# Cross attention's keys: twelve head pairs by seven half products, alternating with four value units

## The chip, the core and the metric

One core of a Trainium2 chip runs the whole program. Times are device microseconds (us). Before the change three runs gave 1630.26, 1631.77 and 1633.85 us, median 1631.77. The engines are PE (TensorE, the matmuls), ACT (ScalarE), DVE (VectorE), POOL (GpSimd) and SP, whose queue issues every DMA.

## The reference, cut to what matters

The program is two layers (cross attention, gated feed forward, grouped attention, a LoRA layer). Only the start changes: the keys, values and queries of the first cross attention, for 8 x 128 = 1024 tokens, 32 heads of 128 and a model width of 512.

```python
x = _rmsnorm(hidden_states, ln_weight)          # hidden_states = _layernorm(x)
h_q = (x @ w_q.T).reshape(b, lq, H, DH)         # H = 32, DH = 128
h_k = (key_value_states @ w_k.T).reshape(b, lk, H, DH)
h_v = (key_value_states @ w_v.T).reshape(b, lk, H, DH)
score = jnp.einsum('bqhd,bkhd->bhqk', h_q, h_k) + position_bias[None]
...
x = x + _L0_xattn_ref(_layernorm(x, axis=-1), ctx_4096, ...)
```

## The kernel before, in words

**Three matmuls for one.** Every float32 product is made of three passes in a rounded format (`product`, L55 to L57): an operand is a pair, `hi` (rounded, a copy on ACT) and `lo` (what is left, a subtraction on DVE or POOL), and the passes are lo x hi, hi x lo, hi x hi. Weights arrive by DMA in `rawA`, `rawB`, `rawV`, `rawO` (128 x 1024 float32 each); ACT writes `wt*_hi`, then POOL `wt*_lo`, and only then does PE use them. There is one buffer for each of the four kinds, so the next split waits until PE has used the last.

**The context stage.** The transposed context is the pair `c_cT`. Eight rounds (`context_round`, written out for 0 and 1, a hardware loop for 2 to 6, the last in pieces) make keys and values of four heads each. A round before has eight key units, four from `wtA` (one head pair) and four from `wtB` (the next), then eight value units (one for each batch, four heads wide, from `wtV` and `wtO`). Every unit is 4 x 3 = 12 matmuls of 512 columns into one PSUM bank. ACT copies key units to `c_k_kept` (`keep_keys`, L837), DVE value units to `c_v_kept` (`keep_value`, L1046), and SP stores both to memory for the later stage. All four banks of the units are shared by keys and values.

**The input.** In round 0 DVE takes the statistics of `resid` (L1026), centres (L1035), ACT scales (L853), PE transposes one batch behind each value unit (`turn_x`, L636), ACT and DVE make `xT_hi` and `xT_lo`. POOL makes the factors: `scale_of` for that scaling, and `twice_of` (five small operations, L1233 to L1241) for `add_hidden` on ACT (L863), which turns `resid` into twice the normalised input, at the end of round 1.

**Seven half products.** The queries of a head pair are made by Strassen's scheme already (`first_five`, `sixth`, `seventh`): the pair's weights and the tokens are halved both ways, four combinations of the weights are made by POOL (`combine`), four of the input once (`Twist`, `x_twist`), and seven half products of 6 matmuls each, some added in the bank, replace four units of 12. ACT copies one quarter twice, DVE forms the sums (`query_sum`, L1116).

**What sets the order.** Every engine has its own list of instructions, written out by hand in the functions `sync`, `tensor`, `scalar`, `vector` and `gpsimd`, and runs it strictly in that order; semaphores hold one engine back for another. So an instruction that waits holds everything behind it on its engine.

Of the kernel before, what the change touches and what calls it, by code (L numbers as in the profile page):

```python
# [19 lines left out]
ALU = mybir.AluOpType  # L20
# [46 lines left out]
class Core:  # L67
# [29 lines left out]
    def place_context(self):  # L97

        self.cT = self.pair(self.ctx, "cT", [P, DC, TOK])
# [156 lines left out]
class Twist:  # L256
# [3 lines left out]
    def __init__(self, core, ctx, tag, nth):  # L260
        self.core, self.nth = core, nth
# [16 lines left out]
    def difference(self, dve, n, of, less, step):  # L278
        dve.wait_ge(self.core.twist_steps, 8 * self.nth + step)
        dve.tensor_tensor(self.plain[n - 1][:, :, :], self.plain[of - 1][:, :, :], self.plain[less - 1][:, :, :],  # L280
                          ALU.subtract).then_inc(self.core.twist_steps, 1)

    def high(self, act, n, step):
        act.wait_ge(self.core.twist_steps, 8 * self.nth + step)
        self.core.nc.scalar.copy(self.parts[n - 1][0][:, :, :], self.plain[n - 1][:, :, :]).then_inc(self.core.twist_hi, 1)
# [19 lines left out]
def cross_attention_phase(core, io, kept, norm_row, after):  # L305
# [9 lines left out]
    with ExitStack() as ctx:  # L315
# [3 lines left out]
        twist = Twist(core, ctx, "x", 0)  # L319
# [27 lines left out]
        ctx_raw = [v_kept[:, h, :, :].rearrange("p b f -> p (b f)") for h in range(4)]  # L347
        ln_w = core.row
# [54 lines left out]
        K_UNITS, V_UNITS = 8 * QUADS, 8 * QUADS  # L403
        CTX_A, CTX_B, CTX_V = QUADS + 1, QUADS, QUADS
# [11 lines left out]
        def x_bank(b):  # L416
            return banks[:, 4 + b % 4, :].rearrange("p (c t) -> p c t", c=DC)
# [7 lines left out]
        def context_rounds(engine, body):  # L425
            body(0)
            body(1)
            with engine.Fori(2, QUADS - 1) as i:
                body(i)

# [7 lines left out]
        def sync(sp):  # L438
# [16 lines left out]
            def store_keys(i, which):  # L455
                sp.wait_ge(qk_copied, 8 * i + 4 * which + 4)
# [9 lines left out]
            def context_round(i):  # L466
                key_weights("A", 2 * i + 2, i + 2)
                key_weights("B", 2 * i + 3, i + 1)
                value_weights(i + 1, i + 1)
                if isinstance(i, int) and i == 0:  # L470
                    small()
                store_keys(i, 0)
                store_keys(i, 1)
                store_values(i, 0)
                store_values(i, 1)

            def small():
                sp.wait_ge(ctx_hi, 2 * DC)
                sp.wait_ge(ctx_lo, 2 * DC)
                for n in range(2):  # L480
                    sp.dma_start(kept["ctx"][n], f32(cT[n][:, :, :]).rearrange("p c t -> p (c t)")).then_inc(ctx_stored, DMA)
                sp.wait_ge(centred_ready, B)
# [81 lines left out]
        def tensor(pe):  # L564
# [4 lines left out]
            def key_unit(kind, i, u):  # L569
                h, half = u % 4 // 2, u % 2  # L570
                if u >= 4:
                    pe.wait_ge(qk_copied, 8 * i + u - 3)
                elif not isinstance(i, int) or i:
                    pe.wait_ge(vo_added, 8 * i + u - 3)
# [21 lines left out]
            def keys(kind, i, which):  # L596
                weights_ready(kind, i + 2 if kind == "A" else i + 1)
                for u in range(4 * which, 4 * which + 4):
                    key_unit(kind, i, u)
# [8 lines left out]
            def value_unit(i, b):  # L608
                if b >= 4:
# [2284 lines left out]
```

## Time and profile before

| what | value |
|---|---|
| median of three runs | 1631.77 us |
| the profiled execution, its own time | 1630.46 us |
| its span | 1628.7 us |
| granted TensorE clock | 1.0 over the whole span |
| busy share of the span: PE, DVE, ACT, POOL | 99%, 58%, 46%, 50% |
| context stage (rounds 0 to 7) on PE | from 6 us to about 348 us |

The profile comes from one execution, whose own time is the number to add to and take from. A busy share near one says that PE has nearly no gap left, so there time can only come from fewer or shorter matmuls, or from one of its few gaps; on the other engines an idle stretch costs nothing unless PE waits for them. Matmuls overlap, so the mean duration of one (about 390 ns) is longer than the distance between two starts, which is what a matmul costs.

### The profile page before, as it was taken

What the parts mean: (1) busy time and instruction counts of PE and PEld (TensorE: products, weight loads), DVE (VectorE), ACT (ScalarE), POOL (GpSimd) and SP (SyncE); (2) the same over time, 40 slices, a digit from 0 to 9 for tenths busy, and PEclk for the clock granted to TensorE, in tenths of its full rate; (3) what the DMA queues carried; (4) which work ended last, traced back from release to release, by engine and by line L of the source; (5) the groups of instructions that cost most, each with busy time, mean ns of one, the idle gap of its engine ahead of it and who ended that gap; (6) DMA issues with size and microseconds to landing.
All of it is one profiled execution on the core that took longest, in us unless ns stands there. A gap on an engine that the chain in (4) does not pass through costs nothing.

```text
span 1628.7 us, 24911 instructions
## 1 busy us (share of the span) xinstructions
PE 1613.7 (99%) x8584; PEld 1377.3 (85%) x8584; DVE 936.5 (58%) x1460; ACT 748.0 (46%) x1930; POOL 814.8 (50%) x628
## 2 busy tenths in 40 slices
PE   9999999999999999999989999999999999999999
PEld 7888888888888888888878887888898898889887
DVE  4621111126567666666669666776657656665675
ACT  5331111115455454554553333656546545554653
POOL 5222212237656566476459775554535535453445
PEclk9999999999999999999999999999999999999999
DMA  8544433323333233332332111110111111010011
GB/s 318 192 151 155 155 129 147 125 89 115 103 107 122 93 118 119 107 120 99 113 130 59 51 48 56 59 33 27 46 33 40 46 39 33 27 36 26 24 53 52
DMA packets 52108, 146.40 MB, mean 90 GB/s; under 512 B 7265, under 2 KB 12001, under 8 KB 51521
## 3 DMA queue, kind: packets, MB, share of 16 engines
q1 hardware_dynamic: 52032, 145.41, 25.8%
q8 instruction: 46, 0.75, 0.2%
q14 instruction: 30, 0.24, 0.0%
HBM read 107.64 MB, written 37.75 MB: 89 GB/s over the span
## 4 chain that ended last, share of the span: by engine, by line
PE 93%; DVE 3%; POOL 1%; DMA 1%; ACT 1%; issue 1%; SPq 0%; DVEq 0%; POOLq 0%; ACTq 0%
PE banks L55 26%; PE banks L57 26%; PE banks L56 26%; PE banks L2053 3%; PE banks L689 3%; PE banks L709 3%; PE banks L698 2%; PE banks L2060 2%; DMA resid<-in_x 1%; PE banks L223 0%; DVE stats L1026 0%; DVE resid L1703 0%; POOL rstd L195 0%; DVE stats L182 0%; PE banks L636 0%
## 5 line engine op out<-in xcount | busy, mean ns | idle before, releaser
L1046 DVE COPY c_v_kept<-banks 128x512 f32<-128x512 f32 x64 | 44.3, 692 | 252.6 <-PE banks L57 252.6
L2517 POOL TENSOR_TENSOR g_swapped<-g_swapped,rawB 128x512 f32<-128x512 f32 x80 | 103.2, 1293 | 171.1 <-ACT g_swapped L2199 171.1
L1297 POOL TENSOR_TENSOR x_probs<-x_probs,x_inv 128x512 f32<-128x512 f32 x64 | 66.7, 1042 | 170.8 <-DVE x_inv L1102 168.0
L903 ACT ACTIVATE x_probs<-x_probs,x_top 128x128 f32<-128x128 f32 x256 | 99.5, 390 | 92.2 <-DVE x_top L1093 92.2
L2347 DVE TENSOR_TENSOR g_turned_by<-banks,rawB 128x512 f32<-128x512 f32 x80 | 55.2, 690 | 87.6 <-ACT g_swapped L2199 87.6
L2511 POOL TENSOR_TENSOR g_probs<-g_probs,g_inv 128x512 f32<-128x512 f32 x64 | 67.7, 1081 | 74.6 <-DVE g_inv L2338 74.4
L55 PE MATMUL banks<-wtV_hi,g_att_lo 128*128 128x512 f32 x256 | 104.3, 407 | 0.0
L55 PE MATMUL banks<-xT_hi,wtO_lo 128*128 128x512 f32 x256 | 102.9, 402 | 0.0
L2198 ACT COPY g_swapped<-banks 64x512 f32<-64x512 f32 x80 | 46.7, 584 | 121.5 <-PE banks L57 114.9
L56 PE MATMUL banks<-wtV_lo,g_att_hi 128*128 128x512 f32 x256 | 100.3, 392 | 0.0
L57 PE MATMUL banks<-xT_hi,wtO_hi 128*128 128x512 f32 x256 | 100.2, 391 | 0.0
L56 PE MATMUL banks<-xT_lo,wtO_hi 128*128 128x512 f32 x256 | 99.9, 390 | 0.0
L57 PE MATMUL banks<-wtV_hi,g_att_hi 128*128 128x512 f32 x256 | 99.8, 390 | 0.0
L55 PE MATMUL banks<-wtO_hi,x_att_lo 128*128 128x512 f32 x240 | 96.2, 401 | 0.0
L1112 DVE TENSOR_TENSOR resid<-banks,resid 128x512 f32<-128x512 f32 x128 | 85.3, 685 | 17.6 <-PE banks L57 17.5
L57 PE MATMUL banks<-wtO_hi,x_att_hi 128*128 128x512 f32 x240 | 93.8, 391 | 0.0
L56 PE MATMUL banks<-wtO_lo,x_att_hi 128*128 128x512 f32 x240 | 93.4, 389 | 0.0
L1116 DVE TENSOR_TENSOR x_q<-banks,x_q 128x512 f32<-128x512 f32 x80 | 55.1, 688 | 59.7 <-PE banks L57 59.2
L2189 ACT ACTIVATE g_probs<-g_probs 128x128 f32<-128x128 f32 x256 | 75.7, 298 | 26.2 <-DVE g_probs L2333 26.2
L2333 DVE SCALAR_TENSOR_TENSOR g_probs<-g_probs,g_cap,rawB 128x512 f32<-128x512 f32 x64 | 77.5, 1213 | 17.6 <-ACT g_probs L2183 17.5
L1212 POOL TENSOR_TENSOR wtA_lo<-rawA,wtA_hi 128x1024 fp32r<-128x1024 f32 (+1 forms) x25 | 57.8, 2310 | 55.5 <-ACT wtA_hi L821 36.7
L2369 DVE TENSOR_TENSOR resid<-banks,resid 128x512 f32<-128x512 f32 x120 | 80.8, 674 | 6.1 <-PE banks L57 5.7
(334 smaller groups left out, 5037.4 us busy)
## 6 DMA issues: line engine op xcount, KB each, us to landing
kept_k<-c_k_kept SPq DMA_DIRECT2D x16, 1024.0 KB, 4.0
x_k<-kept_k SPq DMA_DIRECT2D x32, 512.0 KB, 4.1
kept_v<-c_v_kept SPq DMA_DIRECT2D x14, 1024.0 KB, 5.0
x_v<-kept_v SPq DMA_DIRECT2D x28, 512.0 KB, 4.0
rawA<-in_x_wQ SPq DMA_DIRECT2D x16, 512.0 KB, 4.6
rawO<-in_x_wO SPq DMA_DIRECT2D x16, 512.0 KB, 3.5
rawO<-in_g_wQ SPq DMA_DIRECT2D x16, 512.0 KB, 3.5
rawV<-in_g_wO SPq DMA_DIRECT2D x16, 512.0 KB, 3.4
```

What stands on the lines that cost most here:

```text
L55: pe.matmul(out, w[1], x[0], start=start, stop=False, skip_group_check=adds)
L56: pe.matmul(out, w[0], x[1], start=False, stop=False, skip_group_check=adds)
L57: return pe.matmul(out, w[0], x[0], start=False, stop=stop, skip_group_check=adds)
L903: e = nc.scalar.activation(probs[:, b, :], probs[:, b, :], ACT.Exp, bias=top[:, b:b + 1], accum_out=total[:, b:b + 1])
L1112: dve.tensor_tensor(resid[:, b, :], banks[:, out_bank(g, b), :], resid[:, b, :], ALU.add)\
L1212: return pool.tensor_tensor(wt[into][1][:, cut], raw[kind][:, cut], f32(wt[into][0][:, cut]), ALU.subtract)
L1297: pool.tensor_tensor(probs[:, part, :], probs[:, part, :], rows, ALU.mult).then_inc(probs_ready, 1)
L2189: e = nc.scalar.activation(probs[:, t, :], probs[:, t, :], ACT.Exp, accum_out=total[:, t:t + 1])
L2333: dve.scalar_tensor_tensor(part, part, cap[:, 0:1], wide(mask), ALU.mult, ALU.add)\
L2369: dve.tensor_tensor(resid[:, b, :], banks[:, out_bank(r, u, b), :], resid[:, b, :], ALU.add).then_inc(proj_free, 1)
L2511: pool.tensor_tensor(probs[:, quarter(j), :], probs[:, quarter(j), :], rows, ALU.mult)\
L2517: pool.tensor_tensor(part, part, sin[:, :].unsqueeze(1).to_broadcast([P, HB, P]), ALU.mult)\
```

## The change

**Keys.** The first two head pairs (round 0) and the last two (round 7) are made as before. For the twelve pairs between, the keys are made by seven half products from `wtA` and `wtB` together, with `c_twist`, four combinations of the context that DVE makes in round 0 (`key_differences`) in the memory where `x_twist` lies later. A round from 1 to 6 is now, twice over: seven half products of one pair with one value unit between the fifth and the sixth, then three value units. ACT makes two copies for a pair, DVE five sums (`key_sums`) where ACT made four copies. POOL makes the weight combinations (`combine`) once for each pair, and the weights of a pair are split after the sixth and seventh product of the pair before. The combinations of the input for the queries move from round 1 to the end of round 6 and the time of the last keys.

**Input.** Statistics and centring move behind the first value units on DVE, the scaling behind the eight key copies on ACT; four of the eight transposes stay in round 0 (behind values 4 to 7), four move into round 1. They use banks 6 and 7 where they used 4 to 7; the values of round 1 use banks 4 and 5, those of later rounds 4 to 7. `twice_of` and the mask's conversion (`mask_of`) move on POOL from the end of round 0 to the end of round 1.

**An address.** `cT`, the context as grouped attention reads it again, gets a gap in front, as `c_cT` has one: it starts on a line of 128 bytes now, and 96 bytes into one before.

```diff
     def place_context(self):
 
+        self.line_up(self.ctx, "cT_line")
         self.cT = self.pair(self.ctx, "cT", [P, DC, TOK])
...
+        SEVENS = PAIRS - 4
+        K_UNITS, V_UNITS = 8 + 7 * SEVENS + 8, 8 * QUADS
...
         def x_bank(b):
-            return banks[:, 4 + b % 4, :].rearrange("p (c t) -> p c t", c=DC)
+            return banks[:, 6 + b % 2, :].rearrange("p (c t) -> p c t", c=DC)
+
+        def key_step(i, which):
+            return 2 * i - 2 + which
...
# sync
             def context_round(i):
-                key_weights("A", 2 * i + 2, i + 2)
-                key_weights("B", 2 * i + 3, i + 1)
...
+                key_weights("A", 2 * i + 1, key_step(i, 1) + 2)
                 value_weights(i + 1, i + 1)
...
                 store_keys(i, 0)
+                key_weights("A", 2 * i + 2, key_step(i, 1) + 3)
+                store_values(i, 0)
...
                 store_keys(i, 1)
-                store_values(i, 0)
                 store_values(i, 1)
...
# tensor
+            def seven_keys(i, which):
+                n = key_step(i, which)
+                weights_ready("A", 2 + n + 1)
+                pe.wait_ge(qk_copied, 8 + 2 * n)
+                if isinstance(i, int) and i == 1 and which == 0:
+                    pe.wait_ge(vo_added, 8)
+                    key_twist.ready(pe, 4)
                 else:
-                    pe.wait_ge(qk_copied, 8 * i + 5 + b)
-                value_product(b, b % 4)
+                    pe.wait_ge(q_sums, 5 * n)
+                part(X, a11, c11)
+                part(Y, s2, ct2)
+                part(Z, s1, ct1)
+                pe.wait_ge(qk_copied, 8 + 2 * n + 1)
+                part(X, a12, c21, True)
+                pe.wait_ge(q_sums, 5 * n + 1)
+                part(Y, s3, ct3, True)
+                if which == 0:
+                    weights_ready("V", i + 1)
+                    weights_ready("O", i + 1)
+                value_unit(i, 4 * which)
+                if isinstance(i, int) and i == 1 and which == 0:
+                    turn_x(4)
+                pe.wait_ge(q_sums, 5 * n + 2)
+                part(Y, a22, ct4, True)
+                pe.wait_ge(q_sums, 5 * n + 3)
+                part(Z, s4, c22, True)
...
+                for which in range(2):
+                    seven_keys(i, which)
+                    for b in range(4 * which + 1, 4 * which + 4):
+                        value_unit(i, b)
+                        if isinstance(i, int) and i == 1 and which == 0:
+                            turn_x(b + 4)
...
# scalar
+            def seven_weights(n, loads, a_used, b_used):
+                act.wait_ge(raw_in["A"], DMA * loads)
+                act.wait_ge(w_steps, 4 * n + 2)
+                act.wait_ge(qk_made, a_used)
+                nc.scalar.copy(wt["A"][0][:, :], raw["A"][:, :])
+                act.wait_ge(w_steps, 4 * n + 4)
+                act.wait_ge(qk_made, b_used)
+                nc.scalar.copy(wt["B"][0][:, 0:6 * P], raw["B"][:, 0:6 * P]).then_inc(w_hi["A"], 1)
+
+            def key_weights(n):
+                seven_weights(n, n + 2, products_before(n - 1) + 6, products_before(n))
...
+                value_weights(i)
...
+                key_copy(i, 0)
...
+                key_quarter(i, 0)
...
+                key_weights(key_step(i, 0) + 1)
...
+                key_copy(i, 1)
+                key_quarter(i, 1)
...
+                    key_weights(key_step(i, 1) + 1)
                 if second:
-                    twist.high(act, 2, 6)
-                    twist.high(act, 4, 8)
                     for b in range(B):
                         add_hidden(b)
-                value_weights(i + 1)
...
# gpsimd
             def context_round(i):
...
+                value_weights(i)
+                for which in range(2):
+                    n = key_step(i, which) + 1
...
+                        combine(n, n + 2, ("A", n + 2))
+                        seven_low(n + 3)
+                if isinstance(i, int) and i == 1:
                     twice_of()
-                    pool.wait_ge(mask_in, DMA)
-                    pool.wait_ge(qk_made, 4)
-                    pool.tensor_scalar(mask, mask8, MASKED, -MASKED, ALU.mult, ALU.add).then_inc(mask_ready, 1)
-                value_weights(i + 1)
+                    mask_of()
```

How the lists move at three places, before first and the changed one second. A name ahead of `<-` is written, those behind it are read; in brackets stand the semaphores that it waits for.

**ACT in round 0**, from the last weights of the start to the first transposed input: `c_k_kept` are the key copies, `s_centred` the input.

```order
L821 CAST wtO_hi<-rawO 128x1024 [waits x_raw_inO]
L837 COPY c_k_kept<-banks 128x512 [waits x_qk_made] x4
L821 CAST wtA_hi<-rawA 128x1024 [waits x_raw_inA,x_qk_made]
L853 ACTIVATE s_centred<-s_centred,s_scale 128x512 [waits s_centred_ready,s_scale_ready] x4
L837 COPY c_k_kept<-banks 128x512 [waits x_qk_made] x4
L821 CAST wtB_hi<-rawB 128x1024 [waits x_raw_inB,x_qk_made]
L858 CAST xT_hi<-banks 128x4x128 [waits s_x_turned]
```

```order
L915 CAST wtO_hi<-rawO 128x1024 [waits x_raw_inO]
L928 COPY c_k_kept<-banks 128x512 [waits x_qk_made] x4
L292 CAST c_twist_hi<-c_plain 128x1024 [waits twist_steps] x2
L928 COPY c_k_kept<-banks 128x512 [waits x_qk_made]
L292 CAST c_twist_hi<-c_plain 128x1024 [waits twist_steps] x2
L928 COPY c_k_kept<-banks 128x512 [waits x_qk_made] x3
L961 CAST wtA_hi<-rawA 128x1024 [waits x_qk_made,x_w_steps,x_raw_inA]
L964 CAST wtB_hi<-rawB 128x768 [waits x_qk_made,x_w_steps]
L983 ACTIVATE s_centred<-s_centred,s_scale 128x512 [waits s_centred_ready,s_scale_ready] x4
L988 CAST xT_hi<-banks 128x4x128 [waits s_x_turned] x3
```

The scaling of the input stood between the first four key copies and the last four; now it stands behind all eight, and behind the first split for the seven products.

**ACT from the end of round 1 into round 2** (the branch and the ISA row are the loop's start): `resid` is `add_hidden`, `wtV_hi` and `wtO_hi` the value weights of round 2.

```order
L821 CAST wtB_hi<-rawB 128x1024 [waits x_raw_inB,x_qk_made]
L285 CAST x_twist_hi<-x_plain 128x1024 [waits twist_steps] x2
L863 ACTIVATE resid<-resid,s_mean_scaled,s_twice 128x512 [waits s_twice_ready] x8
L821 CAST wtV_hi<-rawV 128x1024 [waits x_raw_inV,x_vo_made]
L821 CAST wtO_hi<-rawO 128x1024 [waits x_raw_inO]
L428 UNCONDITIONAL_BRANCH
L428 ISA
L836 ISA [waits c_k_stored0]
L837 COPY c_k_kept<-banks 128x512 [waits x_qk_made]
```

```order
L955 COPY c_k_kept<-banks 128x512 [waits x_qk_made]
L961 CAST wtA_hi<-rawA 128x1024 [waits x_qk_made,x_w_steps,x_raw_inA]
L964 CAST wtB_hi<-rawB 128x768 [waits x_qk_made,x_w_steps]
L993 ACTIVATE resid<-resid,s_mean_scaled,s_twice 128x512 [waits s_twice_ready] x8
L451 UNCONDITIONAL_BRANCH
L451 ISA
L914 ISA [waits x_vo_made]
L915 CAST wtV_hi<-rawV 128x1024 [waits x_raw_inV]
L915 CAST wtO_hi<-rawO 128x1024 [waits x_raw_inO]
L949 REGISTER_ALU
L950 ISA [waits c_k_stored0]
L951 COPY c_k_kept<-banks 128x512 [waits x_qk_made]
```

The value weights of round 2 stand behind `add_hidden` in both; the key weights that `add_hidden` stands behind are other ones, and the first key copy of round 2 follows the value weights as before.

**POOL around `twice_of`** (`rstd`, `s_mean_scaled`, `s_twice`): in round 0 before, at the end of round 1 now.

```order
L1212 TENSOR_TENSOR wtA_lo<-rawA,wtA_hi 128x1024 [waits x_w_hiA]
L1212 TENSOR_TENSOR wtB_lo<-rawB,wtB_hi 128x1024 [waits x_w_hiB]
L1233 TENSOR_SCALAR var_eps<-moments 128x8 [waits s_scale_ready]
L1235 TENSOR_TENSOR rstd<-var_eps,power 128x8 [waits s_scale_steps]
L1237 TENSOR_TENSOR var_eps<-moments,rstd 128x8 [waits s_scale_steps]
L1239 TENSOR_SCALAR s_mean_scaled<-var_eps 128x8 [waits s_scale_steps]
L1241 TENSOR_SCALAR s_twice<-rstd 128x8 [waits s_scale_steps]
L1259 TENSOR_SCALAR normed<-row 128x1024 [waits x_qk_made,x_mask_in]
```

```order
L1428 TENSOR_TENSOR wtA_lo<-rawA,wtA_hi 128x1024 [waits x_w_hiA]
L1509 TENSOR_TENSOR wtB_lo<-rawB,wtB_hi 128x768
L1445 TENSOR_SCALAR var_eps<-moments 128x8 [waits s_scale_ready]
L1447 TENSOR_TENSOR rstd<-var_eps,power 128x8 [waits s_scale_steps]
L1449 TENSOR_TENSOR var_eps<-moments,rstd 128x8 [waits s_scale_steps]
L1451 TENSOR_SCALAR s_mean_scaled<-var_eps 128x8 [waits s_scale_steps]
L1453 TENSOR_SCALAR s_twice<-rstd 128x8 [waits s_scale_steps]
L1458 TENSOR_SCALAR normed<-row 128x1024 [waits x_qk_made,x_mask_in]
L451 UNCONDITIONAL_BRANCH
L451 ISA
L1428 TENSOR_TENSOR wtV_lo<-rawV,wtV_hi 128x1024 [waits x_w_hiV]
L1428 TENSOR_TENSOR wtO_lo<-rawO,wtO_hi 128x1024 [waits x_w_hiO]
```

The five small operations stood behind splits of round 0; now they are the last but one thing of round 1, behind the low parts of the weights of its last pair (`wtA_lo`, `wtB_lo`).

## Rows read from the trace of the kernel before

**Rows 1.** The page, part 1: busy us of each engine, share of the span, instructions.

```profile
PE 1613.7 (99%) x8584; PEld 1377.3 (85%) x8584; DVE 936.5 (58%) x1460; ACT 748.0 (46%) x1930; POOL 814.8 (50%) x628
```

**Rows 2.** The waits of PE, whole span: us in total, times, longest.

```profile
PE banks L55 <- ACT c_k_kept L837: 2.4, 1, 2.4
```

**Rows 3.** Timeline of PE, end of round 0's keys: start us, us, engine, line, operation.

```profile
29.08 0.39 PE L57 MATMUL banks<-c_cT_hi,wtB_hi 128*128 128x512 f32 x1
...
31.89 0.47 PE L55 MATMUL banks<-wtV_hi,c_cT_lo 128*128 128x512 f32 x1 [2.42 <-ACT c_k_kept L837]
...
34.70 0.60 PE L636 MATMUL banks<-ident,s_centred 128*128 128x128 f32 x4
```

**Rows 4.** Timeline of ACT, rounds 0 and 1: scaling the input, adding the hidden.

```profile
28.56 2.71 ACT L853 ACTIVATE s_centred<-s_centred,s_scale 128x512 f32<-128x512 f32 x4 [3.50 <-DVE s_centred L1035]
...
82.89 5.75 ACT L863 ACTIVATE resid<-resid,s_mean_scaled,s_twice 128x512 f32<-128x512 f32 x8
```

**Rows 5.** Timeline of DVE, rounds 0 and 1.

```profile
22.44 2.48 DVE L1026 BATCH_NORM_STATS2 stats<-resid 128x6 f32<-128x512 f32 x4 [9.01 <-DMA resid<-in_x]
...
27.74 2.71 DVE L1035 SCALAR_TENSOR_TENSOR s_centred<-resid,moments,row 128x512 f32<-128x512 f32 x4
...
57.33 0.69 DVE L1046 COPY c_v_kept<-banks 128x512 f32<-128x512 f32 x1 [1.46 <-PE banks L57]
...
60.12 7.22 DVE L275 TENSOR_TENSOR x_plain<-xT_hi,xT_lo 128x1024 f32<-128x1024 f32 x3
67.26 3.48 DVE L280 TENSOR_TENSOR x_plain<-x_plain 128x1024 f32<-128x1024 f32 x3
```

**Rows 6.** Timeline of POOL, end of round 0 and start of round 1.

```profile
36.71 0.70 POOL L1233 TENSOR_SCALAR var_eps<-moments 128x8 f32<-128x8 f32 x1
37.50 1.67 POOL L1235 TENSOR_TENSOR rstd<-var_eps,power 128x8 f32<-128x8 f32 x1
...
39.88 0.74 POOL L1241 TENSOR_SCALAR s_twice<-rstd 128x8 f32<-128x8 f32 x1
...
61.74 3.38 POOL L1212 TENSOR_TENSOR wtO_lo<-rawO,wtO_hi 128x1024 fp32r<-128x1024 f32 x1
```

**Rows 7.** Groups of PE by form: count, busy us, mean ns of one.

```profile
L57 PE MATMUL banks<-c_cT_hi,wtB_hi 128*128 128x512 f32 x128 | 49.8, 389 | 0.0
...
L57 PE MATMUL banks<-x_twist_hi,wtB_hi 128*128 128x512 f32 x64 | 25.0, 390 | 0.0
...
L57 PE MATMUL banks<-cT_hi,wtB_hi 128*128 128x512 f32 x64 | 25.3, 395 | 0.0
```

**Rows 8.** Timeline of ACT, a steady round's start and the first query weights.

```profile
275.40 1.05 ACT L821 CAST wtV_hi<-rawV 128x1024 fp32r<-128x1024 f32 x1 [20.23 <-PE banks L57]
...
278.12 0.59 ACT L837 COPY c_k_kept<-banks 128x512 f32<-128x512 f32 x1 [0.72 <-PE banks L57]
280.84 0.59 ACT L837 COPY c_k_kept<-banks 128x512 f32<-128x512 f32 x1 [2.13 <-PE banks L57]
...
342.11 0.83 ACT L929 CAST wtB_hi<-rawB 128x768 fp32r<-128x768 f32 x1
```

**Rows 9.** Timeline of POOL, a steady round's start and the first query weights.

```profile
278.88 2.40 POOL L1212 TENSOR_TENSOR wtO_lo<-rawO,wtO_hi 128x1024 fp32r<-128x1024 f32 x1
...
326.25 0.74 POOL L1271 TENSOR_TENSOR rawB<-rawA 128x256 f32<-128x256 f32 x1 [1.46 <-DMA rawA<-in_x_wQ]
...
328.58 0.74 POOL L1276 TENSOR_TENSOR rawB<-rawA,rawB 128x256 f32<-128x256 f32 x1
343.02 2.40 POOL L1212 TENSOR_TENSOR wtA_lo<-rawA,wtA_hi 128x1024 fp32r<-128x1024 f32 x1 [13.70 <-ACT wtB_hi L929]
345.38 1.85 POOL L1280 TENSOR_TENSOR wtB_lo<-rawB,wtB_hi 128x768 fp32r<-128x768 f32 x1
```

**Rows 10.** Timeline of the DMA queue of SP, weight loads at two round starts.

```profile
277.33 0.37 SPq L443 DMA_DIRECT2D rawA<-in_x_wK  x1
...
320.43 0.37 SPq L443 DMA_DIRECT2D rawA<-in_x_wQ  x1
```

More of the change, by code:

```diff
@@ L746, in first_pair @@
                 value()
+                twist.ready(pe, 4)
                 first_five(0)
@@ L840, in key_weights, with keep_unit, last_keys @@
-            def key_weights(kind, i):
-                act.wait_ge(qk_made, 8 * i + (4 if kind == "A" else 8))
-                split(kind, i + 2).then_inc(w_hi[kind], 1)
+            def keep_unit(u, made):
+                act.wait_ge(qk_made, made + u + 1)
+                nc.scalar.copy(k_kept[:, u // 4, u % 4 // 2, token_half(u % 2)], banks[:, u % 4, :]).then_inc(qk_copied, 1)
+            def last_keys():
+                made = K_UNITS - 8
+                value_weights(QUADS - 1)
+                act.wait_ge(k_stored[0], DMA * (QUADS - 1))
+                keep_unit(0, made)
+                keep_unit(1, made)
+                twist.high(act, 1, 4)
+                keep_unit(2, made)
+                twist.high(act, 3, 5)
+                keep_unit(3, made)
+                twist.high(act, 2, 6)
+                act.wait_ge(k_stored[1], DMA * (QUADS - 1))
+                keep_unit(4, made)
+                twist.high(act, 4, 8)
+                for u in range(5, 8):
+                    keep_unit(u, made)
@@ new lines, in first_round, with keep @@
+            def first_round():
+                for n in range(2 * DC):
+                    context(n)
+                key_differences()
+                def keep(b):
+                    keep_value(0, b, value_bank(0, b))
+                keep(0)
+                statistics(0)
+                keep(1)
+                statistics(1)
+                keep(2)
+                dve.wait_ge(small_in, 2 * DMA)
+                centre(0)
+                centre(1)
+                keep(3)
+                centre(2)
+                centre(3)
+                keep(4)
+                for b in range(5, B):
+                    keep(b)
+                    x_low(b - 5)
+                    centre(b - 1)
@@ new lines, in context_round @@
+                for which in range(2):
+                    n = key_step(i, which) + 1
+                    if isinstance(i, int) and i == QUADS - 2 and which == 1:
+                        split("A", CTX_A).then_inc(w_lo["A"], 1)
+                        split("B", CTX_B).then_inc(w_lo["B"], 1)
+                    else:
+                        combine(n, n + 2, ("A", n + 2))
+                        seven_low(n + 3)
+                if isinstance(i, int) and i == 1:
+                    twice_of()
+                    mask_of()
```

387 lines of the change are left out of this document (247 added, 140 removed).

## The prediction

> **What bounds the kernel now.** I read the page's busy times first: PE is busy 1613.7 of 1628.7 us, 99% [rows 1], so time can only come from matmuls that go or from PE's few gaps. The waits of PE name one gap in the stage that changes, 2.4 us for a key copy of ACT [rows 2]. The timeline of PE puts it behind the keys of round 0: the last key matmul starts at 29.08, the first value matmul at 31.89 [rows 3]. The timeline of ACT says why: it stood at the scaling of the input, 3.50 us idle for DVE's centring, with four key copies queued behind it [rows 4]; DVE could not begin the statistics until `resid` had landed, at 22.44 [rows 5]. From there to the queries PE has no gap. A unit of 12 matmuls takes 2.72 us (two key copies of ACT start at 278.12 and 280.84 [rows 8]), so one matmul costs 0.2267 us and a half product of six 1.36.
>
> **Matmuls removed.** A head pair took 4 x 12 = 48, and takes 7 x 6 = 42. Twelve pairs: 72 fewer, 72 x 0.2267 = 16.3 us, all on PE, which is the path. The half products have the same shape; with the input's combinations the mean of one is 390 ns against 389 for plain context operands [rows 7]. Over 504 matmuls 1 ns is 0.5 us, the bound of that term.
>
> **Round 0.** ACT now copies all eight key units before it scales the input. The two pairs of casts of the context's combinations stand among them, but even so the copy that value 0 needs is the first after two casts, and PE asks for it only at 29.3. So the gap of 2.4 us goes. What is late next is the first transpose, after value 4, at 29.3 + 5 x 2.72 = 42.9. Ahead of it on DVE: copy of value 0 (made at 32.0), half the statistics (27.74 - 22.44 = 5.3 for both halves [rows 5], so 2.65), copy, the other half, copy, one centring (0.7), then ACT's scaling (0.7). From 32.1 that is 41.0, 1.9 us early. DVE may however not be free at 32.1, because eight new operations of 128 x 1024 run against POOL. The trace shows what that does: three such took 7.22 us beside POOL's splits, and POOL's own split took 3.38 where 2.40 is its length [rows 5, 6, 9]; three took 3.48 with POOL idle [rows 5]. By turns like these, against three splits and four combinations of POOL, DVE is free at about 32.9, and the transpose is ready 1.1 us early. Cost 0, at most 1 us. The Trainium skill, page "SBUF — State Buffer", section "SBUF: two separate sides", says that DVE and GpSimd share a port pair as an exclusive lock when a DVE operation has two SBUF inputs; by plain durations instead DVE would be free at 29.9. The trace agrees with the lock (7.22 against 3.48), and either way the sum gets 0 here.
>
> **Start of round 1.** The transposes are a wash: eight before, eight now, about 0.5 us each (31.89 to the copy of value 7 at 57.33 is 25.4 us for 21.8 us of values and seven transposes [rows 3, 5]). Round 0 ends at 29.3 + 21.8 + 4 x 0.5 = 53.1. The first product waits for the copy of value 7, made at 52.6 and copied by 53.4: +0.3 us.
>
> **Start of round 2, the term to look at.** `twice_of` now stands on POOL behind the split of the last pair of round 1, and eight `add_hidden` on ACT wait for it, ahead of the value weights and of the first key copy of round 2, as the two lists in the text on the change show. Step by step:
> - Round 1 is 84 + 96 = 180 matmuls and four transposes, 40.8 + 2.0: from 53.4 to 96.2. The seventh product of its second pair ends three values earlier, at 88.0.
> - ACT's cast of `wtB_hi` takes 0.83 [rows 8]: 88.9. POOL's low parts: 345.38 - 343.02 = 2.36, and 1.85 [rows 9]: 93.1.
> - `twice_of`: from 36.71 to 39.88 + 0.74, 3.9 us, of which about 1 us is two operations held by DVE (0.70 and 0.74 for what is nearer 0.2) [rows 6]. Between 2.9 and 3.9 I take 3.4: 96.5.
> - Eight `add_hidden`, 5.75 us [rows 4]: 102.3. Two casts of value weights to 104.3 (1.05 each, overlapping a little [rows 8]), the key copy to 104.9.
> - PE needs that copy before its fourth product, at 96.2 + 3 x 1.36 = 100.3. It waits 4.6 us. Two products later, at 107.6, it needs `wtO_lo`, which ends 281.28 - 275.40 = 5.9 us after the cast of `wtV_hi` starts [rows 8, 9], at 108.2: 0.6 more.
>
> Together +5.2 us; with 2.9 and 3.9 for `twice_of` 4.7 and 5.7, and 6.5 if POOL's mask conversion or DVE's reduction gets in between. Before, the same eight ran at 82.89 under the values, long done, because `twice_of` had ended in round 0. The Trainium skill, page "Perfetto Trace Analysis", section "GPSIMD Engine Instruction", warns that a GpSimd span is unreliable and start-to-start spacing is better; the five spans add up to 3.6 us, the spacing gives 3.9, and the sum would be 0.2 to 0.5 us longer than mine.
>
> **Steady rounds 2 to 6.** With T as a round's start (the value cast of ACT starts there, 275.40 [rows 8]): weights of the next pair are asked for at T + 2.0 (277.33) and land 5.8 us later (320.43 to 326.25) [rows 9, 10]; the four combinations take 328.58 + 0.74 - 326.25 = 3.1 [rows 9], done at T + 10.9. The seventh product is at T + 9.5 + 2.7 = T + 12.2; cast and low parts end 5.1 later, PE has 8.2 us of values meanwhile: 3 us to spare. `wtO_lo` is there at T + 5.9 and needed after five products at T + 6.8: 0.9 to spare, the narrowest. ACT's key copy ends at T + 2.6, needed at T + 4.1. I cost these at 0. If the cover of 0.9 were gone, each microsecond more costs 1 us in each round. At the end of round 6 and in the last keys DVE has 12 operations of 1.16 for the queries' combinations and POOL some 13 us of splits and combinations; even strictly by turns that is 27 us in the 38 us that PE is busy before it needs them. Cost 0.
>
> **The address.** The 3 x 64 matmuls that stream weights past `cT` in grouped attention have a mean of 395 ns, those past the lined-up `c_cT` 389 [rows 7]. If the address is the reason, 192 x 6 ns = 1.2 us go; if not, 0. I take 1.2, since the operation is otherwise the same.
>
> **Sum.** -16.3 - 2.4 + 0.3 + 5.2 - 1.2 = -14.4 us. The profiled execution took 1630.46 us, 1.8 more than its span, and the change touches nothing outside the span: 1616.1. It lies 1.3 us under the median of the runs (1631.77), so 1616.5 is my number.
>
> **Rivals.**
> - *Round 2 does not wait.* Then 1611. For it: POOL's work on eight columns was seen only once, beside DVE. Against: `add_hidden` alone is 5.75 us, and even with `twice_of` at 0 ACT would come to the key copy at 101.5, 1.2 us late. Chance 0.08.
> - *The value weights are late in every round.* Only 0.9 us covers them; if ACT starts the cast late or POOL is held, 1 us in each of six rounds makes 1622, 2 us makes 1628. For it: the list of POOL is fuller, and in round 1 centring runs between the two splits. Against: in rounds 2 to 6 DVE reads the banks and runs nothing of the kind that held POOL. Chance 0.17.
> - *Slower than before: the pair's weights land late.* Two buffers fed the keys before and one pair's load was asked for a round ahead; now half of the loads are asked for at T + 2.0 and must be combined, cast and subtracted by T + 20.4. From landing on that is 8.3 us, so PE waits once a load takes over 10 us, and at 12.5 us for each (2.4 us in each of six rounds) all 14.4 us are gone. For it: stores of 1 MB are issued just ahead. Against: 5.8 us was measured in such a place [rows 9, 10]. Chance 0.05.
> - *It does not do what it says*, half products costing 10% more each, 504 x 0.023 = 11.6 us: 1628. Against: the equal means of [rows 7]. Chance 0.02.
>
> **Numbers.** 0.68 stay for the forecast, whose own range is 1613 to 1619.5. The range of 1610 to 1624 takes in the first rival and the nearer half of the second. A measurement tells 0.2% (3.3 us) from no change. Faster: 0.68 + 0.08 + nearly all of 0.17, so 0.92; slower 0.05; within 0.2% 0.03.
>
> **What would show it.** PE's wait on a key copy in round 0 is gone. Two waits of PE appear near 100 and 108 us, on the key copy (about 4.6) and on `wtO_lo` (about 0.6), with ACT's eight `resid` rows ending near 102. Rounds 3 to 6 last 40.8 us without a gap. The `cT` matmuls fall to 389 ns. I am wrong if PE waits in every round, if the wait near 100 is under 3 us, or if there is one at the last keys or the first transpose.

## The result, and the profile after

| | before | after |
|---|---|---|
| median of the runs | 1631.01 us (1630.15 to 1633.85, 4 runs) | 1617.86 us (1617.45 to 1618.81, 4 runs) |
| profiled execution | 1630.46 us, span 1628.7 | 1618.12 us, span 1616.3 |
| mean granted clock | 1.000 | 0.997 |

The ratio is 0.9917, interval 0.9902 to 0.9932: 13 us faster. The forecast was 1616.5, so it was 1.4 us too low and inside its range. Between the two profiled executions the difference is 12.3 us, where the sum had 14.4.

First the page of the changed kernel, part 1 (busy us, share of the span, instructions), which answers to [rows 1].

```profile
PE 1601.0 (99%) x8512; PEld 1368.2 (85%) x8512; DVE 998.1 (62%) x1528; ACT 748.2 (46%) x1922; POOL 878.1 (54%) x688
```

PE has 8512 instructions, 72 fewer, and is still 99% busy. DVE and POOL each took on 60 us and more, for the combinations of the context and of the key weights.

The waits of PE in the changed kernel, whole span (engine, line, waited for: us in total, times, longest), the two that lie in the changed stage:

```profile
PE banks L55 <- ACT c_k_kept L951: 4.2, 1, 4.2
...
PE banks L55 <- DVE c_v_kept L1193: 0.5, 1, 0.5
```

The 2.4 us of [rows 2] are gone; a wait of 4.2 us on another key copy (L951 is the copy of a half product) has come. The timeline of PE in the changed kernel (start us, us, engine, line, operation, idle time before) at the end of round 0's keys, answering to [rows 3], and at the start of round 2:

```profile
28.54 0.39 PE L57 MATMUL banks<-c_cT_hi,wtB_hi 128*128 128x512 f32 x1
28.77 0.39 PE L55 MATMUL banks<-wtV_hi,c_cT_lo 128*128 128x512 f32 x1
...
99.81 0.39 PE L57 MATMUL banks<-c_twist_hi,wtA_hi 128*128 128x512 f32 x1
104.40 0.79 PE L55 MATMUL banks<-c_cT_hi,wtA_lo 128*128 128x512 f32 x1 [4.20 <-ACT c_k_kept L951]
104.99 0.63 PE L56 MATMUL banks<-c_cT_lo,wtA_hi 128*128 128x512 f32 x1
...
109.26 0.55 PE L57 MATMUL banks<-c_twist_hi,wtB_hi 128*128 128x512 f32 x1
109.64 0.39 PE L55 MATMUL banks<-wtV_hi,c_cT_lo 128*128 128x512 f32 x1
```

In round 0 values follow keys at 0.23 us, without a gap. Behind the matmul of 99.81 PE stops for 4.4 us (104.40 - 99.81 - 0.23; the 4.20 in brackets is counted from the end of that matmul), where 4.6 were predicted. What was not predicted stands behind it: the next twelve matmuls start about 0.43 us apart instead of 0.227, and take 5.24 us (109.64 - 104.40) instead of 2.72. That is 2.5 us more. The windows of the changed kernel show at what clock they ran (stretch, its length, busy us of PE, PEld, DVE, ACT, POOL, granted clock, DMA share, GB/s):

```profile
100.00:102.00 2.00, 0.20 (x1) 0.00 (x0) 0.00 (x0) 2.00 (x4) 0.00 (x0) 1.00 0.97 280
102.00:104.00 2.00, 0.00 (x0) 0.00 (x0) 0.00 (x0) 2.00 (x3) 1.00 (x1) 0.69 0.26 104
104.00:106.00 2.00, 1.60 (x4) 1.31 (x5) 0.69 (x1) 0.34 (x1) 2.00 (x2) 0.50 0.00 0
106.00:108.00 2.00, 2.00 (x7) 1.52 (x6) 0.00 (x0) 0.59 (x1) 2.00 (x2) 0.50 0.57 152
108.00:110.00 2.00, 2.00 (x7) 1.61 (x6) 0.15 (x1) 0.00 (x0) 1.84 (x4) 0.60 0.78 213
110.00:112.00 2.00, 2.00 (x11) 1.63 (x10) 1.23 (x2) 0.00 (x0) 0.70 (x1) 1.00 0.40 160
```

The granted clock (the third number from the end) falls while PE stands still, is 0.50 (the lower level, 1.2 of 2.4 GHz) from 104 to 108, and is full again from 110. Whether the stop is what brought the clock down, these windows alone don't say; e1, e3, e5 and e7 test it.

Why PE waited: the timelines of ACT and, below it, of POOL in the changed kernel (answering to [rows 4 and 6]).

```profile
88.05 0.83 ACT L964 CAST wtB_hi<-rawB 128x768 fp32r<-128x768 f32 x1 [0.28 <-PE banks L57]
96.23 5.75 ACT L993 ACTIVATE resid<-resid,s_mean_scaled,s_twice 128x512 f32<-128x512 f32 x8 [7.35 <-POOL s_twice L1453]
101.89 1.03 ACT L915 CAST wtV_hi<-rawV 128x1024 fp32r<-128x1024 f32 x1
102.82 1.04 ACT L915 CAST wtO_hi<-rawO 128x1024 fp32r<-128x1024 f32 x1
103.77 0.57 ACT L951 COPY c_k_kept<-banks 128x512 f32<-128x512 f32 x1
```

```profile
88.96 2.39 POOL L1428 TENSOR_TENSOR wtA_lo<-rawA,wtA_hi 128x1024 fp32r<-128x1024 f32 x1 [10.82 <-ACT wtB_hi L964]
91.31 1.84 POOL L1509 TENSOR_TENSOR wtB_lo<-rawB,wtB_hi 128x768 fp32r<-128x768 f32 x1
93.23 0.26 POOL L1445 TENSOR_SCALAR var_eps<-moments 128x8 f32<-128x8 f32 x1
93.58 1.67 POOL L1447 TENSOR_TENSOR rstd<-var_eps,power 128x8 f32<-128x8 f32 x1
...
95.96 0.24 POOL L1453 TENSOR_SCALAR s_twice<-rstd 128x8 f32<-128x8 f32 x1
...
103.00 2.36 POOL L1428 TENSOR_TENSOR wtV_lo<-rawV,wtV_hi 128x1024 fp32r<-128x1024 f32 x1 [5.67 <-ACT wtV_hi L915]
105.31 2.37 POOL L1428 TENSOR_TENSOR wtO_lo<-rawO,wtO_hi 128x1024 fp32r<-128x1024 f32 x1
```

This is the forecast's chain link by link: cast of `wtB_hi` (to 88.9; forecast 88.9), low parts (93.15; 93.1), `twice_of` (96.2; 96.5), eight `add_hidden` (102.0; 102.3), two casts and the key copy (104.3; 104.9). `wtO_lo` ends at 107.7, and PE, slowed down, came for it only at 109.6: the second wait predicted, 0.6 us, did not appear.

A steady round, POOL of the changed kernel and below it PE (answering to [rows 9]; the round starts at T = 225.55 with ACT's cast of `wtV_hi`):

```profile
229.04 2.40 POOL L1428 TENSOR_TENSOR wtO_lo<-rawO,wtO_hi 128x1024 fp32r<-128x1024 f32 x1
233.22 0.74 POOL L1493 TENSOR_TENSOR rawB<-rawA 128x256 f32<-128x256 f32 x1 [1.77 <-DMA rawA<-in_x_wK]
```

```profile
225.27 0.39 PE L55 MATMUL banks<-c_cT_hi,wtA_lo 128*128 128x512 f32 x1
...
232.07 0.39 PE L55 MATMUL banks<-wtV_hi,c_cT_lo 128*128 128x512 f32 x1
```

`wtO_lo` ends at 231.44 = T + 5.9, as worked out. PE comes for it at 232.07 = T + 6.5, not T + 6.8: PE begins the round at 225.27, 0.28 us before ACT's cast, where the working had both at T. So 0.6 us was to spare and not 0.9 (0.7 in the round that starts at 266.27). PE has no wait from 110 us to the queries.

The `cT` matmuls, groups of PE by form in the changed kernel (count, busy us, mean ns), answering to [rows 7]:

```profile
L57 PE MATMUL banks<-wtA_hi,cT_hi 128*128 128x256 f32 x128 | 36.2, 283 | 0.0
...
L57 PE MATMUL banks<-cT_hi,wtB_hi 128*128 128x512 f32 x64 | 24.9, 389 | 0.0
```

And the same forms in the kernel before, where I had read only the second:

```profile
L57 PE MATMUL banks<-wtA_hi,cT_hi 128*128 128x256 f32 x128 | 35.7, 279 | 0.0
...
L57 PE MATMUL banks<-cT_hi,wtB_hi 128*128 128x512 f32 x64 | 25.3, 395 | 0.0
```

The 512-column ones fell from 395 to 389 ns, and twice as many 256-column ones rose from 279 to 283.

The difference by stretches, from the starts of marking instructions of PE in the two traces:

| stretch | before, us | after, us | difference | forecast |
|---|---|---|---|---|
| start to first value matmul | 31.89 | 28.77 | -3.1 | -2.4 |
| to first matmul on the input's combinations | 318.1 | 309.4 | -8.7 | -10.8 |
| to first `cT` matmul of 512 columns | 662.8 | 662.7 | -0.1 | 0 |
| to the end of the span | 615.9 | 615.4 | -0.5 | -1.2 |
| sum | | | -12.4 | -14.4 |

### The profile page after: what moved, and what is told of

Its sections match the earlier page's. It is cut to its first block, busy times and chain, and to the rows that moved or that the text cites. A ratio compares the mean times of both kernels' runs of the same rounds, so it can differ in the third digit from the quotient of the medians.

```text
span 1616.3 us, 25021 instructions
## 1 busy us (share of the span) xinstructions
PE 1601.0 (99%) x8512; PEld 1368.2 (85%) x8512; DVE 998.1 (62%) x1528; ACT 748.2 (46%) x1922; POOL 878.1 (54%) x688
## 4 chain that ended last, share of the span: by engine, by line
PE 94%; DVE 3%; POOL 2%; ACT 1%; issue 1%; DMA 0%; SPq 0%; ACTq 0%; DVEq 0%; POOLq 0%
PE banks L55 27%; PE banks L57 26%; PE banks L56 26%; PE banks L2282 4%; PE banks L783 3%; PE banks L803 3%; PE banks L792 2%; PE banks L2289 2%; PE banks L224 0%; PE banks L734 0%; ACT resid L993 0%; DVE resid L1932 0%; POOL rstd L196 0%; DVE stats L183 0%; ACT x_probs L1055 0%
## 5 line engine op out<-in xcount | busy, mean ns | idle before, releaser
L1428 POOL TENSOR_TENSOR wtA_lo<-rawA,wtA_hi 128x1024 fp32r<-128x1024 f32 (+1 forms) x31 | 72.1, 2326 | 98.5 <-ACT wtB_hi L964 77.5
L57 PE MATMUL banks<-xT_hi,wtO_hi 128*128 128x512 f32 x256 | 100.2, 391 | 0.0
L55 PE MATMUL banks<-wtO_hi,x_att_lo 128*128 128x512 f32 x240 | 96.2, 401 | 0.0
L1327 DVE TENSOR_TENSOR resid<-banks,resid 128x512 f32<-128x512 f32 x128 | 85.3, 685 | 17.6 <-PE banks L57 17.5
L1331 DVE TENSOR_TENSOR c_k_kept<-banks,c_k_kept 128x512 f32<-128x512 f32 x60 | 41.5, 692 | 81.6 <-PE banks L57 74.6
```

The source lines that it names most:

```text
L55: pe.matmul(out, w[1], x[0], start=start, stop=False, skip_group_check=adds)
L57: return pe.matmul(out, w[0], x[0], start=False, stop=stop, skip_group_check=adds)
L1327: dve.tensor_tensor(resid[:, b, :], banks[:, out_bank(g, b), :], resid[:, b, :], ALU.add)\
L1331: dve.tensor_tensor(dst, banks[:, bank, :], kept_sum, ALU.add).then_inc(q_sums, 1)
L1428: return pool.tensor_tensor(wt[into][1][:, cut], raw[kind][:, cut], f32(wt[into][0][:, cut]), ALU.subtract)
```

## The experiments

The question behind e1, e3, e5 and e7 is what the wait near 100 us costs, and what makes the matmuls behind it slow. My theory, A: the chain from `twice_of` over `add_hidden` to the key copy causes both, about 6.7 us together, and with the wait gone or short the clock stays full (A1 where an expectation parts this from the wait alone). Executions of one kernel differ by 1 us and more outside the stage that changes (in the profiles the first value matmul of the changed kernel and its variants starts between 28.8 and 29.5 us, and the stretch from the input's combinations to grouped attention takes 662.7 to 663.4). So the worth of an edit is read from the stretch that it changes, from the first value matmul to the first matmul on the input's combinations: 309.4 us in the changed kernel, 318.1 before. Each expectation says itself what its rival makes of the run.

### e1: `twice_of` back at the end of round 0

```diff
@@ POOL, round 0, behind scale_of(1)
+                    twice_of()
                     return
@@ POOL, round 1
                 if isinstance(i, int) and i == 1:
-                    twice_of()
                     mask_of()
```

> The changed kernel with `twice_of` moved on POOL from the end of round 1 to the end of round 0, behind the second `scale_of`; nothing else moves. Theory A (the waits of round 2 come from `add_hidden` standing behind `twice_of` on ACT, and the slow matmuls behind the wait come from the wait): the 4.2 us wait of PE at about 100 us goes, the twelve matmuls behind it take 0.227 us each again instead of 5.2 us for all twelve, and the granted clock stays 1.0 there; together 4.2 + 2.5 = 6.7 us less than the changed kernel, about 1611.2. Rival B (the lower clock there has another reason, the load of the stage): only the wait goes, 4.2 us, about 1613.7, and matmuls of 0.43 us stand somewhere near 104 us still. Rival C (ACT is late for another reason, say the mask conversion or the transfers): the wait stays over 2 us.

Measured: 1612.40 us (1612.04 to 1613.32), ratio to before 0.9888 (0.9873 to 0.9903), 18.5 us under before on the same chip; clock 1.000. The timeline of ACT in e1:

```profile
89.22 5.76 ACT L993 ACTIVATE resid<-resid,s_mean_scaled,s_twice 128x512 f32<-128x512 f32 x8
96.66 1.05 ACT L915 CAST wtV_hi<-rawV 128x1024 fp32r<-128x1024 f32 x1 [1.69 <-PE banks L57]
...
98.57 0.58 ACT L951 COPY c_k_kept<-banks 128x512 f32<-128x512 f32 x1
```

The same eight `add_hidden` run at 89.22 without waiting, and the key copy starts at 98.57. PE waits nowhere there, and its stretch from first value to the input's combinations is 302.5 us against 309.4 in the changed kernel: 6.9 us. Theory A. The median is 1.2 us above the 1611.2 expected: outside that stretch this execution was about 1 us slower than the changed kernel's (values start at 29.20, 0.4 later, and 663.4 us follow where there were 662.7).

### e3: `twice_of` stays, `add_hidden` goes to the end of round 6

```diff
-                if second:
-                    for b in range(B):
+                if isinstance(i, int) and i == QUADS - 2:
+                    for b in range(0, B):
                         add_hidden(b)
```

> The changed kernel with `twice_of` left where it is, but the eight `add_hidden` of ACT moved from the end of round 1 to the end of round 6, ahead of the value weights of round 7. Theory A (what costs is not that POOL is late but that ACT's queue waits for it): the same gain as with an early `twice_of`, about 6.7 us, 1611.2, and at the end of round 6, where ACT has about 6 us free for operations of 5.75 us, no wait of PE over 0.5 us. Rival B (the value weights are late by themselves): a wait of PE of 0.5 to 1 us at the value weights of round 2 remains. Rival D (the eight operations are too long at their new place too): a new wait of 1 us or more near the last keys.

Measured: 1612.07 us (1611.84 to 1612.17), ratio 0.9884 (0.9869 to 0.9899), 18.8 under before; clock 1.000. The timeline of ACT in e3, at the new place:

```profile
294.29 5.76 ACT L993 ACTIVATE resid<-resid,s_mean_scaled,s_twice 128x512 f32<-128x512 f32 x8
300.55 1.05 ACT L915 CAST wtV_hi<-rawV 128x1024 fp32r<-128x1024 f32 x1 [0.50 <-PE banks L57]
```

The value cast behind them still waited 0.50 us for PE, so they cost nothing there. The same 302.5 us as in e1, with `twice_of` where the change put it: what costs is not POOL's late step by itself but ACT standing behind it with the key copy in its queue. Theory A from the other side.

### e5 and e7: only four, or six, of the `add_hidden` in round 1

```diff
 (e5; e7 has 6 for 4)
-                    for b in range(B):
+                    for b in range(4):
+                        add_hidden(b)
+                if isinstance(i, int) and i == QUADS - 2:
+                    for b in range(4, B):
                         add_hidden(b)
```

> The changed kernel with four of the eight `add_hidden` at the end of round 1 and four at the end of round 6: the wait of PE in round 2 should be 4.2 - 4 x 0.72 = 1.3 us. Theory A1 (the clock falls only behind a long wait): the twelve matmuls behind it keep 0.227 us, the granted clock stays 1.0, and the kernel takes 2.9 + 2.5 = 5.4 us less than the changed one, about 1612.5. Rival A2 (any wait at this place brings the lower clock): 2.9 us less, about 1615, with matmuls of 0.43 us behind the wait.

Measured: 1614.19 us (1614.05 to 1614.91), ratio 0.9897 (0.9882 to 0.9912), 16.7 under before; clock 1.000. PE in e5:

```profile
102.36 0.50 PE L55 MATMUL banks<-c_cT_hi,wtA_lo 128*128 128x512 f32 x1 [1.39 <-ACT c_k_kept L951]
...
105.03 0.39 PE L57 MATMUL banks<-c_twist_hi,wtB_hi 128*128 128x512 f32 x1
105.93 0.49 PE L55 MATMUL banks<-wtV_hi,c_cT_lo 128*128 128x512 f32 x1 [0.52 <-POOL wtO_lo L1431]
```

The first wait is 2.8 us shorter (four times 0.72), and the matmuls behind it run at full clock. With PE at full speed the second wait, on `wtO_lo`, is there with 0.52 us: the term that the forecast had and the changed kernel's trace did not show. The number was missed: 1612.5 was expected of A1 and 1615 of A2, and 1614.19 lies nearer to the rival's. It is the trace that decides for A1, with its clock of 1.00 through both waits. The stretch from first value to the input's combinations takes 305.0 us, 4.4 less than in the changed kernel where 5.4 was expected: the second wait (0.7 by starts) had been left out of the sum, and behind a wait twelve matmuls take 2.9 us and not 2.72 even at full clock. The rest of the miss lies outside the stretch (values start at 29.52).

> The changed kernel with six of the eight `add_hidden` at the end of round 1 and two at the end of round 6: the wait of PE in round 2 should be 4.2 - 2 x 0.72 = 2.8 us, between the 1.4 us of four (clock stayed 1.0) and the 4.2 us of eight (clock fell). Theory A1 (there is a length of wait beyond which the clock falls, and it lies between 1.4 and 4.2): either 1.4 us less than the changed kernel with slow matmuls behind the wait, about 1616.5, or 1.4 + 2.5 = 3.9 us less with full-speed ones and a second wait of 0.5 us on `wtO_lo`, about 1614.5. The wait of 2.4 us in the kernel before brought no lower clock, so I expect the second.

Measured: 1616.36 us (1615.54 to 1616.79), ratio 0.9914 (0.9899 to 0.9929); profiled at 1615.54, clock 1.000. PE in e7:

```profile
103.24 0.50 PE L55 MATMUL banks<-c_cT_hi,wtA_lo 128*128 128x512 f32 x1 [2.79 <-ACT c_k_kept L951]
...
105.91 0.39 PE L57 MATMUL banks<-c_twist_hi,wtB_hi 128*128 128x512 f32 x1
106.80 0.49 PE L55 MATMUL banks<-wtV_hi,c_cT_lo 128*128 128x512 f32 x1 [0.50 <-POOL wtO_lo L1431]
```

After a wait of 2.79 us the clock stayed full, and twelve matmuls took 2.9 us. The profiled run is 3.3 us under the profiled run of the changed kernel on that chip (1618.85). By the stretch from first value to the input's combinations it is 3.0 us under the changed kernel (306.4 against 309.4). The median, 1616.36, is only 2.1 under and meets the number of the other case in the expectation, 1616.5, a shorter wait with slow matmuls; the 1614.5 that I expected was missed by 1.9. Two of its four runs had a mean clock of 0.999 and 0.998 and took 1616.7 and 1616.8. In those the clock may have fallen behind the wait after all, or elsewhere; there is no trace of them, so e7 shows what one execution does, and not where the boundary lies.

### c0: the changed kernel once more, on the chip of e2, e6 and e7

> The changed kernel unaltered, run beside the three others of this call so that they are compared on one chip. Every theory: about 1617.9 us, a wait of PE of 4.2 us on the key copy at about 100 us and matmuls of 0.43 us behind it. If the wait is there without the slow matmuls, the lower clock is not tied to it.

Measured: 1618.51 us (1617.00 to 1618.92), ratio 0.9923 (0.9908 to 0.9939). The windows of c0 around the wait:

```profile
104.00:106.00 2.00, 1.45 (x4) 1.16 (x5) 0.69 (x1) 0.50 (x2) 2.00 (x2) 0.50 0.00 0
...
108.00:110.00 2.00, 2.00 (x6) 1.52 (x6) 0.00 (x0) 0.10 (x1) 1.92 (x3) 0.50 0.76 246
```

The wait is 4.2 us again and the clock 0.50 behind it, here until 110.3. The stretch from first value to the input's combinations is 309.7 us. So the slow matmuls are no accident of one execution. That every execution has them is not shown: of the four runs the three at a mean clock of 0.997 or 0.998 took 1618.2 to 1618.9, the one at 0.999, of which there is no trace, took 1617.0.

### e2: the changed kernel without the aligned place of `cT`

```diff
-        self.line_up(self.ctx, "cT_line")
         self.cT = self.pair(self.ctx, "cT", [P, DC, TOK])
```

> The changed kernel without the gap ahead of `cT`, so that it starts 96 bytes into a line of 128 again. Theory A (the address sets what a matmul that streams past `cT` costs): the 192 matmuls of 512 columns have a mean of 395 ns again instead of 389, and those 384 of 256 columns, which were 279 to 281 ns before the change and 283 to 285 after it, go back as well. Net effect by the starts of the first and the last 512-column matmul on `cT` (505.4 us apart before the change, 505.0 after): 0.4 us longer, 1618.3. Rival B (as forecast: only the 512-column ones matter): 1.2 us longer. Rival C (the address does nothing, the means follow something else): no mean changes.

Measured: 1619.03 us (1617.77 to 1619.36), ratio 0.9929 (0.9915 to 0.9942), 0.5 over c0. Groups of PE by form in e2:

```profile
L57 PE MATMUL banks<-wtA_hi,cT_hi 128*128 128x256 f32 x128 | 35.7, 279 | 0.0
...
L57 PE MATMUL banks<-cT_hi,wtB_hi 128*128 128x512 f32 x64 | 25.3, 395 | 0.0
```

Both means are back at the values of before, so the address sets both. So are the distances between starts, which are what a matmul costs: 233.3 ns at 512 columns and 117.5 at 256 in e2 and before, 227.0 and 120.5 in c0 and the changed kernel. From the first `cT` matmul to the end of the span e2 takes 615.8 us, c0 and the changed kernel 615.4: 0.4 us is the worth of the line. The medians differ by 0.5, inside the spread of either kernel; it is the traces that show the 0.4.

### e4: the kernel before, with ACT scaling the input behind its key copies

```diff
-                if first:
-                    for b in range(4):
-                        scale_x(b)
                 if second:
                     twist.high(act, 1, 4)
                     twist.high(act, 3, 5)
                 keep_keys(i, 1)
+                if first:
+                    for b in range(4):
+                        scale_x(b)
```

> The kernel before the change with one line moved: ACT scales the first four batches of the input behind all eight key copies of round 0, not between the first four and the last four. Theory A (the gap of 2.4 us before the first value unit is ACT's queue standing at the scaling): the gap goes, 2.4 to 2.6 us less than before, about 1628.5. Rival B (the gap only moves): the first transpose, behind value 0, waits for the scaled input by 1 us or more, and 1.5 us or less is gained. Rival C (nothing): the gap was also kept open by something else, and stays.

Measured: 1628.28 us (1627.65 to 1629.01, 11 runs), ratio 0.9983 (0.9974 to 0.9992): 2.6 us. The end of round 0's keys on PE in e4:

```profile
29.56 0.39 PE L57 MATMUL banks<-c_cT_hi,wtB_hi 128*128 128x512 f32 x1
29.79 0.39 PE L55 MATMUL banks<-wtV_hi,c_cT_lo 128*128 128x512 f32 x1
```

The gap of [rows 2] is gone by that alone, and it has not moved: from the first value matmul to the last transpose e4 takes as long as before, within 0.1 us. So 2.4 of the changed kernel's 13 us come from the order of ACT's list and need no half product.

### e6: e1, and the first product of round 1 waits for seven value copies instead of eight

```diff
 (on top of e1)
-                    pe.wait_ge(vo_added, 8)
+                    pe.wait_ge(vo_added, 7)
                     key_twist.ready(pe, 4)
```

> The changed kernel with `twice_of` at the end of round 0, and with the first product of round 1 waiting for seven copied values instead of eight (its banks X, Y and Z held values 4 to 6; value 7 is in the fourth bank). Theory A: the wait of PE of 0.5 us on the value copy at 53 us goes too, so 0.5 us less than with the early `twice_of` alone, and 6.5 to 7 us less than the changed kernel on the same chip. Rival B (PE waits at the same place for the context's combinations or the weights instead): the 0.5 us stays under another name.

Measured: 1611.23 us (1610.31 to 1611.62), ratio to before 0.9881 (0.9866 to 0.9896), 7.3 us under c0 on the same chip, where 6.5 to 7 was expected; clock 0.999. No wait on `c_v_kept` is left, and the stretch from first value to last transpose is 45.56 us against 46.32 in e1. It is the fastest kernel of this study. By that stretch it is 0.8 us better than e1; the medians (1612.40 for e1, on another chip) can't be compared so closely.

## Why the prediction was right

Each term beside what was measured:

- **Matmuls removed, -16.3.** Right. The kernel e1 has all of the change except the misplaced step; from first value to the input's combinations it is 15.6 us shorter than before (318.1 - 302.5). With the 0.5 us of round 1's start added back that is 16.1; in e6, where that wait is gone too, the stretch is 16.4 us shorter than before. A half product's matmul costs what a whole one's does: 389 ns in the undisturbed groups, starts 0.227 us apart.
- **Round 0, -2.4.** Right, and shown twice, by the changed kernel and by e4. The first value matmul came at 28.77 where I had 29.3, because this execution's keys started with less of a wait (before, 0.15 us on `c_cT_lo` and 0.35 us on `wtA_lo` up to 8.8 us; here neither); that is the -3.1 in the table of stretches, and 0.7 of it is chance. DVE was free earlier than I had said. Its timeline in the changed kernel, answering to [rows 5]:

```profile
17.14 6.76 DVE L288 TENSOR_TENSOR c_plain<-c_v_kept,c_plain 128x1024 f32<-128x1024 f32 x2
23.83 6.25 DVE L296 TENSOR_TENSOR c_twist_lo<-c_plain,c_twist_hi 128x1024 fp32r<-128x1024 f32 x4
```

  Against POOL's long splits two operations took 6.76 us, 3.4 each. Against POOL's short combinations four took 6.25, 1.6 each, and POOL paid too: a combination took 1.25 to 1.71 us where it takes 0.74 alone. DVE was done at 30.1, not 32.9. The 30.1 is near the 29.9 that the prediction gives for plain durations, but this does not speak for them: a single operation takes 1.2 us, and three of the first four took 3.3 to 3.4. It changed nothing, since value 0 came at 31.8; no transpose waited.
- **Start of round 1, +0.3.** Measured 0.5 (wait on `c_v_kept`), and e6 takes it away; there the stretch gets 0.8 us shorter.
- **Start of round 2, +5.2.** The mechanism was right, with every link within 0.6 us; the size was off by two errors against each other. The wait was 4.4 by starts (forecast 4.6). The second wait, 0.6, was hidden. And 2.5 us came on top, which the prediction put at nothing by leaving it out: it gave the matmuls behind the wait their full speed, and they ran at the lower clock. Together 6.9 instead of 5.2. e1 and e3 take all of it away by two different edits, and by the same 6.9 us.
- **Steady rounds, 0.** Right; the rivals of late value weights and late pair weights did not come. A round lasts 40.8 us (225.27 to 266.07), as forecast. The narrowest cover was 0.6 us and not 0.9, because PE begins a round 0.2 to 0.3 us before ACT's cast. The load asked for at 186.57 landed by 192.22, 5.65 us later where I had 5.8.
- **Queries' combinations, 0.** Right. DVE ended the last of them at 325.2, PE asked from 338.15 on.
- **The address, -1.2.** Too large by 0.8. The step that failed is "192 x 6 ns": I worked out one form and left out the 384 matmuls of 256 columns that use the same `cT`. The prediction also has the sides of the first form the wrong way round: in those 192, `cT` is what streams, 512 columns of it past 128 x 128 weights, and in the 384 it is the stationary operand, which 256 columns of weights stream past. The busy sums give -1.2 + 1.5. By starts the 192 gain 6.3 ns each (-1.2 us) and the 384 lose 3.0 each (+1.2), so the two forms cancel within 0.1; the net of -0.4 that is measured over the whole stage comes for the rest from small differences among its other matmuls, and why those have them is open.

In sum -14.4 became -12.4 by spans: 1.7 on round 2, 0.8 on the address, 0.2 on round 1, less 0.7 for the earlier start. That the forecast came within 1.4 us is in part luck: the slow matmuls that it lacked were offset by the hidden second wait and by the earlier start. The first rival (no wait in round 2, 1611) did not happen in the changed kernel. Its price was nearly that of e1, 1612.4.

## What to carry over

When a step is moved to a later place on one engine, look for the in-order queue that waits for it, and for what stands in that queue behind the waiting instruction: here 6.9 of about 19 us (12.4 + 6.9) were given back because eight operations whose result nobody needed until much later waited for five small ones, with a key copy behind them. A stall of TensorE should be priced with the matmuls behind it: in three profiles the lower clock behind a wait of 4.2 us made twelve of them cost 2.5 us more, in three profiles with waits of 1.4 to 2.8 us in the same stage the clock stayed full. Where an operand's address is changed, count every form that uses the operand, as moving and as stationary side.

## What the runs showed of the hardware that was not expected

- **The clock behind a stop of PE.** Full behind waits of 2.42 (before), 1.39 (e5) and 2.79 us (e7), each in one profile; 0.50 for 5 to 6 us of PE's work behind 4.2 us, in all three profiles with that wait (the changed kernel, c0, e2), and full there where the wait was taken out (e1, e3). The length of the wait is not all there is to it. In the changed kernel the clock fell at 102.7, when PE had stood still since 100.2; in e7 PE stood still from 100.45 to 103.24 at full clock. And in the stage that normalises, PE waits 1.9 us for `normed` in all of these kernels. The window with what follows, in the changed kernel and below it in e1:

```profile
824.00:828.00 4.00, 4.00 (x18) 3.25 (x18) 2.75 (x7) 2.57 (x4) 1.35 (x5) 0.70 0.02 7
```

```profile
818.00:822.00 4.00, 4.00 (x24) 3.28 (x23) 2.73 (x7) 2.57 (x4) 1.34 (x5) 1.00 0.02 6
```

  The clock falls there in the changed kernel, c0, e2 and e6, 0.7 to 1.0 us after PE has started again, and stays full in before, e1, e3, e4, e5 and e7. It costs nothing: from the first matmul of that stage to the first `cT` matmul of 512 columns it is 178.7 us in before, the changed kernel and e1 alike. Two waits of PE that follow take up the slower matmuls: 0.39 us on `normed` and 1.40 on `xT_lo` in before are nothing and 0.41 in the changed kernel. What decides whether the clock falls was not found.
- **The address of a matmul's operand acts both ways:** with the aligned start 395 to 389 ns where `cT` streams (512 columns), 279 to 283 ns where it is stationary (256 columns stream past it); e2 takes both back. Why was not tried.
- **DVE and POOL slow each other, as if by turns of whole operations:** an operation of DVE that takes 1.2 us alone took 3.3 to 3.4 beside POOL's splits (2.4 alone, 3.4 there) and 1.8 beside POOL's combinations (0.74 alone, up to 1.7 there). Each took about its own length and the other's.
